# A three-layer graph network kernel: layer 1 of the last four spans by gathered rows, begun behind the first building slots

## What is computed

```python
# block 1, three times, with one set of GRU weights and weight[l] per layer
m   = x @ weight[l]
agg = segment_sum(m[src] * edge_weight[:, None], dst)     # weighted adjacency times m
x   = gru_cell(agg, x, w_ih, w_hh, b_ih, b_hh)
x   = layernorm(x0 + x)
# block 2, three times
x   = relu((x + segment_sum(x[src], dst)) @ W[l].T + b[l])  # adjacency of counts
out = layernorm(x1 + x)
```

## Time and profile before

| | us |
|---|---|
| median of 3 runs | 2881.55 (2880.4 to 2884.32) |
| the profiled execution, its time | 2883.43 |
| the profiled execution, its span | 2881.7 |
| building, first to last product of L1240 | 27.0 to 989.8 |
| layers 2 and 3 and block 2 | 1014 to 2881.7 |

### The profile page before, as it was taken

One profiled execution on the slowest core, in us unless ns is written; L12 is line 12 of the kernel. 1 busy time (PEld: TensorE's weight loads), 2 busy tenths in 40 slices (PEclk: granted clock), 3 DMA queues, 4 the chain that ended last, 5 costly groups with the idle time before them and its releaser, 6 DMA issues.

```text
span 2881.7 us, 72532 instructions
## 1 busy us (share of the span) xinstructions
PE 2832.6 (98%) x29387; PEld 1881.3 (65%) x29387; DVE 1246.0 (43%) x2716; ACT 947.4 (33%) x1891; POOL 872.5 (30%) x1007
## 2 busy tenths in 40 slices
PE   6999999999999999999999999999999999999998
PEld 5899999999999955555555555555655555555554
DVE  7678877777888514344422344343500010001011
ACT  6777777777777610000001011101400010001111
POOL 4344344443444315554541454544000000000000
PEclk7999999999999999999999999999999999999999
DMA  5666666666662398998996988988487868886884
GB/s 196 267 262 244 245 261 261 257 241 251 262 263 95 113 397 342 350 339 326 355 369 253 340 338 331 357 330 327 149 326 301 310 248 301 309 304 247 318 304 163
DMA packets 134009, 810.64 MB, mean 281 GB/s; under 512 B 17208, under 2 KB 27308, under 8 KB 113948
## 3 DMA queue, kind: packets, MB, share of 16 engines
q1 hardware_dynamic: 111228, 758.32, 67.9%
q0 software_dynamic: 19968, 40.46, 4.4%
q10 hardware_dynamic: 2720, 10.62, 0.9%
HBM read 553.01 MB, written 256.33 MB: 281 GB/s over the span
## 4 chain that ended last, share of the span: by engine, by line
PE 95%; issue 2%; DVE 1%; ACT 1%; DMA 1%; another core or an unknown queue 0%; POOL 0%; DVEq 0%; SPq 0%; ACTq 0%; POOLq 0%
PE ps L969 29%; PE ps L1165 27%; PE ps L1247 19%; PE ps L1240 11%; PE ps L979 1%; PE ps L980 1%; PE ps L1260 1%; PE ps L1261 1%; PE ps L982 1%; PE ps L981 1%; PE ps L1144 1%; ACT ring L1661 0%; DMA sum_rows<-ring 0%; PE ps L1266 0%; PE ps L1267 0%
## 5 line engine op out<-in xcount | busy, mean ns | idle before, releaser
L969 PE MATMUL ps<-ring,Y 128*128 128x448 f32 x2352 | 888.4, 539 | 0.0
L1165 PE MATMUL ps<-ring,Y 128*128 128x448 f16 x4116 | 780.6, 352 | 0.0
L1661 ACT ACTIVATE ring<-ps 128x490 f16<-128x490 f32 (+1 forms) x1344 | 698.3, 651 | 176.7 <-PE ps L1240 169.1
L969 PEld LDWEIGHTS ps<-ring,Y 128*128 128x128 f32 x2352 | 446.4, 190 | 434.8 <-issue 434.8
L1165 PEld LDWEIGHTS ps<-ring,Y 128*128 128x128 f16 x4116 | 402.7, 98 | 373.8
L863 POOL DMA_INDIRECT ring<-y_rows,ring x448 | 431.4, 963 | 518.9 <-PE ps L969 257.7
L1247 PE MATMUL ps<-ring,Y 128*128 (+1 forms) x2744 | 570.2, 360 | 0.4 <-ACT shared L1620 0.4
L1247 PEld LDWEIGHTS ps<-ring,Y 128*128 128x128 f32 x2744 | 503.6, 190 | 8.4 <-ACT shared L1620 0.8
L1240 PEld LDWEIGHTS ps<-shared 64*128 64x128 bf16 x18816 | 320.4, 93 | 76.6 <-issue 59.3
L1240 PE MATMUL ps<-shared 64*128 64x49 bf16 (+1 forms) x18816 | 346.5, 189 | 20.0 <-issue 9.6
L1824 DVE TENSOR_SCALAR ring<-ring 128x128 f32<-128x128 f32 x446 | 130.9, 294 | 388.7 <-DMA ring<-y_rows,ring 205.0
(11 more groups left out here) (196 smaller groups left out, 1450.6 us busy)
## 6 DMA issues: line engine op xcount, KB each, us to landing
ring<-adj_w SPq DMA_DIRECT2D x72, 2688.0 KB
ring<-adj_h SPq DMA_DIRECT2D x42, 2800.0 KB, 9.4
ring<-adj_h SPq DMA_DIRECT2D x42, 2688.0 KB, 9.2
adj_w<-ring SPq DMA_DIRECT2D x48, 2016.0 KB, 11.9
adj_h<-ring SPq DMA_DIRECT2D x56, 1372.0 KB, 5.4
ring<-adj_w SPq DMA_DIRECT2D x24, 2912.0 KB
adj_w<-ring SPq DMA_DIRECT2D x48, 728.0 KB, 6.8
sum_rows<-ring SPq DMA_DIRECT2D x62, 448.0 KB
```

The costliest lines, as they stand in the source:

```text
L969: mm = pe.matmul(ps[:, bank, 0:GW], Y[:, h, :], slab(s)[:, :, h - h0, :], start=(h == 0), stop=(last and h == TILES - 1))
L1165: mm = pe.matmul(ps[:, par, 0:GW], part[:, h, :], counts_slab(par, s)[:, :, h - h0, :], start=(h == 0 and part is Y_high), stop=(h == TILE ...
L1661: act.activation(strip[:, :, c0:c0 + UNIT * WIN].rearrange("p h (d j) -> p d h j", d=WIN)[:, :, :, w0:w1], psum_unit(a)[:, :, kind, :, :]. ...
```

## The change

Layer 1 of the spans 24 to 27 is done by gathered rows too. For that:

1. The building starts with these four spans (`ORDER`). Their slots 0 to 3 build counts only (`build_counts`): 28 products of 49 columns a batch for 84, no L2143, three evictions for six, two column steps on GpSimd for seven, and no `add_tiles`.
2. In slots 5 to 24 the 224 rounds of rows of x are fetched by GpSimd (`fetch_batch`, 11 or 12 a slot by `BATCH_ROWS`), scaled by ScalarE two batches later (`scale_rows`), summed by VectorE four batches later (`sum_batch`), and stored from ScalarE's queue five batches later, 4 rounds at a time (`store_sums`). The 16 end gathers come in slots 26 and 27. The rows live in 16 buffers of their own (`run_bufs`), summed in place.
3. The layer-1 order is `GATE_ORDER`: spans 0 to 22, 24 to 27, 23. Slot t adds span t-5 and does the gates of span t-6; behind the building stand the tiles of span 23 in six parts, five gates and four `flip_run`.
4. In GpSimd's order `near_rows` and its gather move ahead of `take_places`, and the two edge gathers wait for the begin of batches 3 and 5. The loops over slots on DVE, ACT, POOL and SP are written out.
5. Layers 2 and 3 use the same 16 buffers: stores of 4 rounds instead of 7 (54 on SP's queue and 2 on GpSimd's, per layer), and GpSimd now waits for a store where VectorE did.

```diff
-ROW_BUFS = 10
-STORE = 7
+RUN_BUFS = 16
+STORE = 4
...
+FIRST_RUN = GATHERS - RUN_SPANS
+ORDER = [*range(FIRST_RUN, GATHERS), *range(FIRST_RUN)]
+GATE_ORDER = [*range(FIRST_RUN - 1), *range(FIRST_RUN, GATHERS), FIRST_RUN - 1]
+LAST_STORES = 2
+SCALE_LAG, SUM_LAG, STORE_LAG = 2, 4, 5
+PLACE_SLOT, ENDS_SLOT = 25, 26
...
+TAIL_TILES = [0, 6, 15, 24, 33, 42, TILES]
...
+RUN_SLOTS = range(RUN_SPANS + 1, GATHERS - 3)
+BATCH_ROWS = [2, 2, 1, 1, 2, 1, 0, 2]
+MORE_AT, MORE_EVERY = 6, 5
...
-        KEYS_AT, STEPS_AT, LEAPS_AT = 2, 3, 5
+        KEYS_AT, STEPS_AT, LEAPS_AT = 2, 3, 0
...
-        NEAR_AT = 7
+        NEAR_AT = 2
...
+            def fetch_round(turn, i):
+                if i >= RUN_BUFS:
+                    if i % STORE == 0:
+                        use, q = divmod(i // STORE - STORE_TURNS, STORE_TURNS)
+                        pool.wait_ge(s_stored[q], stored_by(turn, q) + 16 * (use + 1))
+                    pool.wait_ge(s_acc, RUN * turn + i - RUN_BUFS + 2)
+                pool.indirect_dma_start(out=run_bufs[:, i % RUN_BUFS, :], out_offset=None, in_=y_rows if turn else x,
+                                        in_offset=bass.IndirectOffsetOnAxis(ap=run_edges[:, i, 0:1].bitcast(I32), axis=0))\
+                    .then_inc(s_row[i % RUN_BUFS], 16)
...
+            def prepare_span(t):
+                par = t % 2
+                n = BATCHES * t
+                fetch_batch(n)
+
+                pool.wait_ge(s_key, OWN_TILES + KEY_STEPS * (t + 2))
+                pool.wait_ge(s_colp, t + 1)
+                pool.sem_inc(s_mark_pool, 1)
+                add_own(t + 1, 1 - par)
+                fetch_batch(n + 1)
+                near_rows(t + 3, 1 - par)
+                batch_begun(n + NEAR_AT)
+                gather_near(1 - par)
+                fetch_batch(n + 2)
+                take_places(t + 2, par)
+                batch_begun(n + FETCH_AT[0])
+                gather(par, 0)
+                fetch_batch(n + 3)
+                fetch_batch(n + 4)
+                batch_begun(n + FETCH_AT[1])
+                gather(par, 1)
+                fetch_batch(n + 5)
+                make_columns(t + 1, 1 - par, n + 6)
+                fetch_batch(n + 7)
...
+            def scale_rows(n):
+                for i in rounds_at(n):
+                    row = run_bufs[:, i % RUN_BUFS, :]
+                    act.wait_ge(s_row[i % RUN_BUFS], 16 * (i // RUN_BUFS + 1))
+                    act.activation(row, row, ACT.Copy, scale=run_edges[:, i, 1:2]).then_inc(s_prod if i else s_acc, 1)
...
+            def sum_row(turn, i):
+                done = RUN * turn + i
+                row, last = (run_bufs[:, j % RUN_BUFS, :] for j in (i, i - 1))
+                dve.wait_ge(s_acc, done)
+                dve.wait_ge(s_prod, done - turn)
+                dve.scalar_tensor_tensor(out=row, in0=last, scalar=run_edges[:, i, 2:3], in1=row,
+                                         op0=ALU.mult, op1=ALU.add).then_inc(s_acc, 1)
```

More of the change, by code:

```diff
@@ L81 @@
 SPAN = WIN * LANES
+RUN_SLOTS = range(RUN_SPANS + 1, GATHERS - 3)
+BATCH_ROWS = [2, 2, 1, 1, 2, 1, 0, 2]
+MORE_AT, MORE_EVERY = 6, 5
+SLOT_ROWS = [[n + (k == MORE_AT and s % MORE_EVERY == 0) for k, n in enumerate(BATCH_ROWS)] for s in range(len(RUN_SLOTS))]
+assert sum(map(sum, SLOT_ROWS)) == RUN
+ENDS = 2 * WIN * RUN_SPANS
 STRIP_BATCHES = SUB // WIN // BATCH
@@ L453, in sums_made, with stored_by, has_weights, hot_steps @@
         def sums_made(b):
-            return run_sums[:, b % 2 * STORE:(b % 2 + 1) * STORE, :]
-        def end_buf(span, d, part):
-            return 2 * (WIN * span + d) + part
-        assert end_buf(RUN_SPANS, 0, 0) <= ROW_BUFS + SUM_BUFS
+            return run_bufs[:, b % STORE_TURNS * STORE:(b % STORE_TURNS + 1) * STORE, :]
+        def stored_by(turn, q):
+            by_sp = [len(range(q, STORES, STORE_TURNS)), len(range(q, STORES - LAST_STORES, STORE_TURNS))]
+            return 16 * sum(by_sp[min(t, 1)] for t in range(turn))
+        def has_weights(t):
+            return t >= GATHERS or ORDER[t] < FIRST_RUN
+        def hot_steps(t):
+            return HOT if has_weights(t) else 2
+        def evictions(t):
+            return EV if t < 0 or has_weights(t) else 1
+        def hot_before(t, k=0):
+            return BATCHES * sum(map(hot_steps, range(t))) + k * hot_steps(t)
+        def evicted(t, k=0):
+            return UNITS * (EV + BATCHES * sum(map(evictions, range(t))) + k * evictions(t))
+        def column_steps(t):
+            return COL_STEPS if has_weights(t) else 2
+        def columns_before(t):
+            return sum(map(column_steps, range(t)))
+        def gates_at(t):
+            return t - RUN_SPANS - 2 if t >= RUN_SPANS + 2 else None
+        def rounds_at(n):
+            slot, k = divmod(n, BATCHES)
+            if slot not in RUN_SLOTS:
+                return range(0)
+            s = RUN_SLOTS.index(slot)
+            first = sum(map(sum, SLOT_ROWS[:s])) + sum(SLOT_ROWS[s][:k])
+            return range(first, first + SLOT_ROWS[s][k])
+        def ends_at(n):
+            slot, k = divmod(n, BATCHES)
+            if slot < ENDS_SLOT:
+                return range(0)
+            first = (slot - ENDS_SLOT) * sum(BATCH_ROWS) + sum(BATCH_ROWS[:k])
+            return range(min(first, ENDS), min(first + BATCH_ROWS[k], ENDS))
         def in_pairs(v):
@@ L844, in _ @@
-            with pool.Fori(0, GATHERS // 2 - 3) as i:
-                prepare_spans(i)
-            for i in range(GATHERS // 2 - 3, GATHERS // 2):
-                prepare_spans(i)
+            def fetch_round(turn, i):
[7 more added lines that the diff above has]
+                    .then_inc(s_row[i % RUN_BUFS], 16)
@@ new lines, in fetch_end, with fetch_ends @@
+            def fetch_end(span, d, part):
+                pool.indirect_dma_start(out=run_bufs[0:LANES, end_buf(span, d, part), :], out_offset=None, in_=sum_rows,
+                                        in_offset=bass.IndirectOffsetOnAxis(ap=run_ends[:, part, d, span:span + 1], axis=0))\
+                    .then_inc(s_ends[span], 16)
+            def fetch_ends(turn):
+                for b in range(STORES - LAST_STORES, STORES):
+                    pool.wait_ge(s_acc, RUN * turn + STORE * (b + 1))
+                    pool.dma_start(sums_kept(b), sums_made(b)).then_inc(s_last, 16)
+                for q in range(STORE_TURNS):
+                    pool.wait_ge(s_stored[q], stored_by(turn + 1, q))
+                pool.wait_ge(s_last, 16 * LAST_STORES * turn)
+                for e in range(ENDS):
+                    fetch_end(e // (2 * WIN), e // 2 % WIN, e % 2)
@@ L849, in _ @@
+            for t in range(GATHERS):
+                prepare_span(t)
             pool.wait_ge(s_steps, WIN * (GATHERS + 2))
@@ L896, in _ @@
                     fetch_rows(layer)
-                    fetch_ends(layer)
+                    fetch_ends(1 + layer)
             with pool.Else():
@@ L1234, in build_unit @@
                             sums = psum_unit(a)[:, d, :, w - w0, :]
-                            if part == 0:
+                            if not weighted:
+                                rhs = hot[slots, buf, 0, w, 0:TILES]
+                                sums = sums[:, 0, :]
+                            elif part == 0:
                                 rhs = hot[slots, buf, 0:2, w, 0:TILES]
```

524 lines of the change are left out of this document (278 added, 246 removed).

## The result

The changed kernel takes 2887.17 us (median; the kernel before 2881.55 in its first three runs), a ratio of 1.002 with an interval of [1.0011, 1.0028]: slower by 0.2%, just at what can be told from no change. The forecast was 2848.5 us, in a range of 2815 to 2880, and so a gain of 1.1%. The profiled execution took 2885.33 us, its span 2883.6.

The account below looks back on a forecast made before the run. TensorE was taken to bound the kernel, busy throughout the steady building. From the profiled span 2881.7 us: building -70, behind it +11, row work +26, layers 2 and 3 0, sum -33; forecast 2848.5 us, range 2815 to 2880.

Parts of the forecast that it names:

- Count slots: Slots 0 to 3, counts only: 19 us a slot, about 79 us with the first weighted span's columns.
- behind the building: From the last building product to layer 2: 41 us for 30, by four more gate sets and flips, +11.
- layers 2 and 3: Same bytes, finer stores: cost taken as 0; 5 to 20 us if slabs or ends come late.
- Slots 4 and 5: Slot 4 without tiles or gates 27 us, slot 5 without gates 32 us.
- Structure: Whole kernel with reordered spans, before any row work: -59 us, 2822.5 us.
- DVE and ACT: Slots 5 to 24: sums 3.9 us a slot on DVE, scalings 0.4 us each on ACT, both hidden.
- A round: One row gather on POOL: 1.25 us start to start; upper bound, half of them held 0.3 longer, +76.
- TensorE: nothing: Row work in slots 5 to 24: adds nothing to TensorE's own work.
- These slots are bound by POOL and DVE in turn, and TensorE waits at the first batch of each: Slots 5 to 24: 1.7 us more a slot, taken as 1.3, +26 in all.
- The sum 35.9: Slots 5 to 24: DVE 8.9, POOL's own steps 18.2, seven rounds 8.8 us, against TensorE's 34.2.
- the ring: Slots 5 to 24: DVE needs POOL's columns, POOL makes them after DVE's keys; 35.9 us once around.
- The rival of the slower side: Slots 5 to 24: every round meets DVE's L2140 or L2143; 1.55 a round, 38.0 a slot, 2898 us; chance 0.14.

Follow-up runs that it names:

- x1: Changed kernel without layer 1's row work in the building (no gathers, scalings or sums; stores kept): 2827.44 us.
- x2: Changed kernel without the 224 row gathers of layer 1; scalings, stores and sums kept: 2829.19 us.
- x3: Changed kernel with the 224 row gathers and stores kept, scalings and sums left out: 2867.89 us.
- x14: x7 with only the unused gather behind batch 3 of each slot, 20 in all: 2835.17 us.
- x15: Kernel before the change, a span's first edge gather also waiting for the fourth tile behind batch 2: 2885.29 us.
- x16: Changed kernel, rows also in slots 2 to 4, at most nine or ten a slot later, end gathers in slot 27: 2860.68 us.
- x18: x16 with 21 more semaphore increments on GpSimd and 13 on ScalarE ahead of slot 0: 2858.55 us.
- x9: Changed kernel with rows per batch [1,1,1,1,3,0,1,3] and batch 6's row fetched behind the columns: 2941.07 us.
- x6: x1 plus 80 row gathers nobody uses, four a slot, each waiting for the first tile behind its batch: 2854.07 us.
- x8: x7 with each of the 80 gathers replaced by a plain transfer of as many bytes: 2829.52 us.
- x7: x6 with each of the 80 gathers waiting for the fifth tile instead of the first: 2867.48 us.

## Why the prediction was wrong

- *Count slots, behind the building, layers 2 and 3*: right (77.6 for 79, 40.9 for 41, 0.3 for 0). Slots 25 to 27 too.
- *Slots 4 and 5*: 66.4 for 59. Most of that is structure, since x1, which gathers no rows there, took 63.9. Seven tiles took 3.79 us in slot 5 (from 136.56) for the usual 2.92, and lengthened batches were in no term.
- *Structure*: 2822.5 forecast, 2827.4 measured (x1), most of it in slots 4 and 5.
- *DVE and ACT*: right that the sums and scalings hide (x2 against x1, 1.8 us); a scaling took 435 ns for 400. That holds without gathers. Without scalings and sums the gathers cost 40 us (x3) and with them 60, so some 18 us come only with both; VectorE's work makes gathers longer, but no run took that apart.
- *A round*: "1.25 from start to start" measured 1.52. The upper bound (1.25 + 0.3) was nearly the right value. The Trainium skill's page "SBUF — State Buffer" (A bandwidth-pool intuition that's wrong) has a transfer issued by GpSimd wait until VectorE lets go of the port that they share; its section Who interferes with whom excepts a tensor_tensor, by an inference. The traces are with the first: x14's gather of 1.76 us began beside a tensor_tensor, and between 200 and 884 us the rows took 1218 ns for the 0.94 of the earlier trace rows. They don't agree in every case: the gather of x15 at 321.91 began beside one, too, and took 1.00.
- *The step that failed* is the first under the row work, "TensorE: nothing". Gathers on GpSimd lengthened TensorE's products: these hold 53.5 of the 59.0 us that slots 6 to 24 took over 34.2 each, and 2.5 where no row is gathered (x2). It was taken for nothing because TensorE has no instruction for a row, and because the one row that spoke against it, the 1.78 at 987.99, was used as a time stamp only.
- *"These slots are bound by POOL and DVE in turn, and TensorE waits at the first batch of each"*: 1.9 us in 19 slots for 24.7. The sum 35.9 counted GpSimd's steps as a chain without end; in fact they wait for TensorE's batches several times a slot, and what a row took was first taken from those waits. Only in x16 to x18 does the ring bind.
- The rival of the slower side had nearly the right size (a round of 1.52 for 1.25, and 2898 for the 2887 measured) and the wrong place, so its size came out by luck; by its own text the slots would lose at batch 0.

What stays open: why gathers leave TensorE alone in x16 to x18; why some batches are lengthened whose gather had ended before them (x9); and what it is in a gather that stops TensorE. For the last, a stop of the supply of instructions fits the gaps at places where the program has no wait, but no run separates it from another stop of TensorE's sequencer.

## What to carry to other kernels

Before a gather by addresses is put on GpSimd "because it has time", look in TensorE's timeline for a place where one already runs beside the small matmuls, and compare the row's duration with its neighbours: here one row of 1.78 us among hundreds of 1.51 pointed to a cost of some 50 us. A row of a profile that is used for its start has a duration, too. And take a stage apart with the first experiments (no work, no gathers, gathers alone): these three told that the 60 us come only with one kind of instruction, while the five kernels in which I rearranged the rows by a theory all missed their forecast, until one worked for a reason that I hadn't given.

## What the runs showed of the hardware

- Beside gathers, TensorE's signals were seen late as well. In the changed kernel batch 4 of a slot is through at 638.31, where its tiles start; ScalarE's eviction of its last unit and VectorE's next batch, which both wait for that unit, start at 642.57, put down to "remote", behind three gathers in a row:

```profile
638.29 1.03 POOL L893 DMA_INDIRECT run_bufs<-in_x,run_edges  x1 [0.30 <-issue]
638.31 2.58 PEld L1335 LDWEIGHTS ps<-ring,Y 128*128 128x128 f32 x14
...
640.87 0.94 POOL L893 DMA_INDIRECT run_bufs<-in_x,run_edges  x1 [0.30 <-issue]
...
642.57 0.90 ACT L1803 ACTIVATE ring<-ps 128x392 f16<-128x392 f32 x2 [1.71 <-remote]
642.57 0.52 DVE L2290 TENSOR_TENSOR shared<-iota_key,shared 128x700 bf16<-128x700 bf16 x1 [3.65 <-remote]
```

- The gather by addresses that waited for the landing of one begun at 432.89 began at 441.93, 9.0 us later (x6), so a wait for the last gather is no small thing.
- A plain transfer of the same 64 KB takes 0.57 us of GpSimd (x8, median), a gather by addresses 0.94 to 2.0 (x7).
- What a gather costs TensorE depends on what runs beside it: in the changed kernel the seven tiles from 676.77 take their 2.92 us beside two gathers (from 676.99 and 678.52), while 84 small products take 1.68 to 1.71 us for 1.44 (x14).
